# Experts of a mixture-of-experts stage: 28 pairs of token tiles with stationary weights, then 15 single tiles

## What is computed

```python
NUM_EXPERTS, TOP_K, HIDDEN, INTER = 8, 2, 256, 704
xf = layernorm(x).reshape(4096, HIDDEN)
top_w, sel = jax.lax.top_k(xf @ w_router.T, TOP_K)
top_w = jax.nn.softmax(top_w, axis=-1)
gates = zeros((4096, 8)).at[arange, sel].add(top_w)
for e in range(8):
    h = silu(xf @ w_gate[e]) * (xf @ w_up[e])
    out = out + gates[:, e:e + 1] * (h @ w_down[e])
x = x + out
```

## Time and profile before

| | |
|---|---|
| median of 3 runs | 1516.23 us |
| the profiled execution | 1514.07 us, span 1512.0 us |
| TensorE busy in the span | 1418.8 us (94%) |
| VectorE, ScalarE, GpSimd busy | 1119.2, 1002.8, 833.8 us |
| attention, scan and router | to 991 us |
| experts, first product to the end | 1003 to 1512 us |

### The profile page before, as it was taken

The page is one execution under the profiler, slowest core; times in us unless marked ns, Lnnn a source line. Parts: engine busy times, 40 slices in busy tenths (PEclk is TensorE's granted clock), DMA queues, the critical chain, the costliest instruction groups (busy, mean ns, idle before and its releaser), DMA issues.

```text
span 1512.0 us, 54304 instructions
## 1 busy us (share of the span) xinstructions
PE 1418.8 (94%) x15668; PEld 1285.3 (85%) x15669; DVE 1119.2 (74%) x3999; ACT 1002.8 (66%) x2482; POOL 833.8 (55%) x1401
## 2 busy tenths in 40 slices
PE   6969999999999999999999999559999999999997
PEld 5858888888888888888888888459999999999997
DVE  3647877877877877877877877558777777787775
ACT  4626777677777767767767766147767677677674
POOL 3514655655655665665665654236666656566554
PEclk9969999999999999999999999569999999999999
DMA  6202454454343343343343231425555555555554
GB/s 189 71 21 72 139 180 129 145 186 129 104 112 91 100 116 91 97 119 91 92 120 95 83 83 31 183 97 145 160 145 151 155 143 159 136 144 162 143 143 111
DMA packets 102009, 183.81 MB, mean 122 GB/s; under 512 B 19392, under 2 KB 61376, under 8 KB 101792
## 3 DMA queue, kind: packets, MB, share of 16 engines
q1 hardware_dynamic: 86272, 164.35, 35.8%
q0 software_dynamic: 15680, 18.76, 7.0%
HBM read 152.63 MB, written 31.13 MB: 122 GB/s over the span
## 4 chain that ended last, share of the span: by engine, by line
PE 70%; DVE 10%; issue 7%; DMA 2%; POOL 2%; ACT 1%; DVEq 1%; POOLq 0%; ACTq 0%; SPq 0%
PE k L412 12%; PE m L412 10%; PE y_p L1474 9%; PE up_p L1474 9%; PE gate_p L1474 8%; PE v_p L412 6%; PE sc L412 5%; PE v_p L476 4%; PE pt L476 3%; PE ht_p L1513 3%; DVE kT L873 2%; DMA par<-zbuf,gi 2%; PE m L497 2%; DVE z L1031 1%; PE z_p L1480 1%
## 5 line engine op out<-in xcount | busy, mean ns | idle before, releaser
L738 ACT ACTIVATE wd<-wd,nmx 128x257 f32<-128x257 f32 x512 | 256.3, 504 | 35.3 <-DVE nmx L884 30.6
L714 ACT ACTIVATE wd<-v_p 128x512 f32<-128x512 f32 x256 | 152.6, 596 | 180.8 <-PE k L412 146.3
L884 DVE CUSTOM_DVE_ANT_0 wd<-sc,wd 128x257 f32<-128x257 f32 x512 | 192.2, 423 | 74.2 <-PE sc L412 69.5
L1301 POOL TENSOR_TENSOR ctx_lo<-wd,ctx_hi 128x516 fp32r<-128x516 f32 x128 | 166.9, 1304 | 138.3 <-ACT ctx_hi L714 138.3
L1676 POOL DMA_INDIRECT out<-par,oi x71 | 113.6, 1599 | 144.8 <-ACT par L1582 140.0
L412 PE MATMUL k<-ctx_hi,wkh 128*128 128x256 f32 x512 | 159.0, 311 | 1.7 <-POOL ctx_lo L1301 1.4
L1553 ACT ACTIVATE uw_hi<-wu 128x1408 fp32r x71 | 98.4, 1385 | 83.7 <-PE up_p L1474 83.4
L1664 POOL COPY oi<-par 128x4 int32 x71 | 148.1, 2086 | 0.0
L1611 DVE TENSOR_TENSOR uw_lo<-wu,uw_hi 128x1408 fp32r<-128x1408 f32 x71 | 115.5, 1626 | 41.2 <-ACT uw_hi L1553 41.2
L412 PE MATMUL k<-ctx_lo,wkh 128*128 128x256 f32 x512 | 145.4, 284 | 0.0
L412 PE MATMUL k<-ctx_hi,wkl 128*128 128x256 f32 x512 | 144.7, 283 | 0.0
(11 more groups left out here) (200 smaller groups left out, 4719.2 us busy)
## 6 DMA issues: line engine op xcount, KB each, us to landing
dl<-d_low SPq DMA_DIRECT2D x71, 768.0 KB, 4.4
wd<-in_ctx SPq DMA_DIRECT2D x128, 258.0 KB, 2.8
wd<-in_mask SPq DMA_DIRECT2D x512, 32.1 KB, 1.8
wd<-in_wd SPq DMA_DIRECT2D x24, 256.0 KB, 3.0
d_high<-wd SPq DMA_DIRECT2D x24, 256.0 KB
d_low<-wd SPq DMA_DIRECT2D x24, 256.0 KB
wd<-d_high SPq DMA_DIRECT2D x8, 768.0 KB, 9.2
wg<-in_wg SPq DMA_DIRECT2D x8, 704.0 KB
```

Of the source, the lines that this page charges most:

```text
L714: return nc.scalar.activation(out, in_, ACT.Copy, **kw)
L738: nc.scalar.activation(pr[:, g, :], sm[:, g, :], ACT.Exp, bias=nmx[:, g:g + 1], scale=-1.0, accum_out=rsum[:, g:g + 1]).then_inc(exp_done, 1)
L884: V.tensor_tensor_reduce(sm[:, g, :], SC[g][:, 0:S], msk[:, b, :], -1.0, 3.0e38, ALU.add, ALU.min, nmx[:, g:g + 1]).then_inc(max_done, 1)
L1301: G.tensor_tensor(ctx_lo[:, b % 2], ctx[:, b], ctx_hi[:, b % 2].bitcast(F32), ALU.subtract).then_inc(lo_done, 1)
```

## The change

The 71 tiles become 28 pairs (NPAIR) of two tiles of one expert, and 15 single tiles (NSLOT) that are worked on as before. The planner finds for each expert how many pairs it has, takes the first 28, and lists what is left as single tiles: 25 VectorE steps, of which not all wait for the one in front, four small transposes and two copies.

For a pair, gate and up are computed with the weights stationary and the 256 rows of z streamed. The result is h already transposed, so h needs no transposes. It comes in six chunks: five of 128 channels with 12 matmuls of 256 columns for gate and up together in one PSUM bank, and a last one in which 64 gate and 64 up channels share one stationary operand (6 matmuls). There are three banks. For each chunk ScalarE takes silu (`silu2`), VectorE the product (`gate_up2`), ScalarE the high half of h (`high_h`), VectorE the low half (`low_h`). The weights of an expert are split once a pair, in parts: the first two chunks (`high_a`, `low_a`, 128x512 for gate and for up), chunks 2 to 4 (`high_b`, `low_b`, 128x768 each) and the short chunk (128x128 each), laid out with gate and up channels in turn. The down product runs as before for each half of a pair, 18 matmuls of 256 columns, in `down_pair`. The low half of w_down is loaded once a pair into one buffer (`load_pair`). Gathers and scatters stay at 128 rows, two a pair, with one copy of slot rows for both. y of a pair has one buffer for each half, and `take_y2` waits for the scatter of the pair before from that buffer, and for `oi` of its pair.

In the diff `body2` is written for TensorE, ScalarE and GpSimd; VectorE's has ScalarE's order with the low halves and products. Lines left out are the buffers, the split of the weights and changed names of semaphores.

```diff
...
-NSLOT = (TOK * TOPK + E * (P - 1)) // P
-assert NSLOT % 2 == 1
+NPAIR = (TOK * TOPK // P - E) // 2
+NSLOT = (TOK * TOPK + E * (P - 1)) // P - 2 * NPAIR
+NTILE = NPAIR + NSLOT
...
-        PLAN = 10
+        PLAN = 25
...
-            for k in range(2):
-                last = mm(M[0:1, (k + 1) * P:(k + 2) * P], tl[:, 3 + k:4 + k], ident)
+            for k in range(4):
+                last = mm(SC[0][0:1, k * P:(k + 1) * P], tl[:, 4 + k:5 + k], ident)
...
+                def step(ins, then=0):
                     k[0] += 1
                     ins.then_inc(plan, 1)
-                    if k[0] < PLAN:
-                        dve.wait_ge(plan, k[0])
+                    if then:
+                        dve.wait_ge(plan, then)
...
+                rows = SC[0][0:1, :].rearrange("p (k n) -> p k n", k=4)
+                V.tensor_copy(info[0:1, :, 0:NPAIR], rows[:, 0:2, 0:NPAIR]).then_inc(info_done, 1)
+                V.tensor_copy(info[0:1, :, NPAIR:NTILE], rows[:, 2:4, 0:NSLOT]).then_inc(info_done, 1)
...
+        def pairs(eng, body):
+            body(0, 0)
+            body(1, 1)
+            with eng.Fori(2, NPAIR - 2, 2) as p:
+                body(p, 0)
+                body(p + 1, 1)
+            body(NPAIR - 2, 0)
+            body(NPAIR - 1, 1)
...
+        def slot(s, k):
+            return 2 * s + k if k < 2 else k + 2
...
+            def turn_pair(p, s):
+                pe.wait_ge(zg_in[s], 32 * (turn(p, s) + 1))
+                at_least(pe, z_done, p)
+                for a in range(NH):
+                    for h in range(2):
+                        o = a * F2 + h * P
+                        last = nc.tensor.transpose(Z2[:, o:o + P], zg2[:, s, h, a * P:(a + 1) * P], ident)
+                last.then_inc(z_ready, 1)
...
+            def chunk(p, s, k):
+                if k == 0:
+                    pe.wait_ge(z_done, p + 1)
+                    pe.wait_ge(a_low, SPLIT_A * (p + 1))
+                if k == 2:
+                    pe.wait_ge(b_low, SPLIT_B * p + 2)
+                if k == FULL:
+                    pe.wait_ge(b_low, SPLIT_B * (p + 1))
+                at_least(pe, hf_done, FC * p + k - 2)
+                (zh, zl), (wh, wl) = zT2[s], w2
+                for side in range(1 if k == FULL else 2):
+                    o = 2 * k * P + side * P
+                    for c in range(NH):
+                        for j, (w, z) in enumerate(((wh, zh), (wh, zl), (wl, zh))):
+                            last = mm(G2[k % 3][:, side * F2:(side + 1) * F2], w[:, c, o:o + P], z[:, c, :],
+                                      c == 0 and j == 0, c == NH - 1 and j == 2)
+                last.then_inc(gu_ready, 1)
+            def down_pair(p, s):
+                e = nc.tensor.value_load(pair_expert(p), min_val=0, max_val=E - 1)
+                pe.wait_ge(h_low, FC * (p + 1))
+                pe.wait_ge(dl2_in, 16 * (p + 1))
+                for h in range(2):
+                    at_least(pe, yp_done, 2 * p + h - 1)
+                    for c in range(FC):
+                        r, at = rows_of(c), slot(s, c)
+                        hh, hl = (x[r, at, h * P:(h + 1) * P] for x in hT2)
+                        wh, wl = wd[r, bass.ds(e, 1), c, :].rearrange("p o n -> p (o n)"), dl2[r, c, :]
+                        for j, (a, b) in enumerate(((hh, wh), (hh, wl), (hl, wh))):
+                            last = mm(Y2[h], a, b, c == 0 and j == 0, c == FC - 1 and j == 2)
+                    last.then_inc(yp_ready, 1)
+            def body2(p, s):
+                chunk(p, s, 0)
+                chunk(p, s, 1)
+                if not (isinstance(p, int) and p == 0):
+                    down_pair(p - 1, 1 - s)
+                if final(p):
+                    turn_z(0, 0)
+                else:
+                    turn_pair(p + 1, 1 - s)
+                for k in range(2, FC):
+                    chunk(p, s, k)
...
+            turn_pair(0, 0)
             pe.wait_ge(wd_in, 16 * E)
+            pairs(pe, body2)
+            down_pair(NPAIR - 1, 1)
+            pe.wait_ge(info_done, 2)
...
+            def silu2(p, k):
+                r = rows_of(k)
+                act.wait_ge(gu_ready, FC * p + k + 1)
+                at_least(act, hf_done, FC * p + k)
+                nc.scalar.activation(sg2[r, :], G2[k % 3][r, 0:F2], ACT.Silu).then_inc(sg_done, 1)
+            def high_h(p, s, k):
+                r = rows_of(k)
+                act.wait_ge(hf_done, FC * p + k + 1)
+                if k < 2:
+                    if not (isinstance(p, int) and p < 2):
+                        act.wait_ge(yp_ready, 2 * p - 2)
+                else:
+                    at_least(act, yp_ready, 2 * p)
+                high(hT2[0][r, slot(s, k), :], hf[k % 2][r, :], h_high)
+            def take_y2(p, s, h):
+                act.wait_ge(yp_ready, 2 * p + h + 1)
+                act.wait_ge(oi_done, p + 1)
+                if not (isinstance(p, int) and p == 0):
+                    act.wait_ge(y_out, 16 * (2 * p + h - 1))
+                nc.scalar.activation(yb2[:, h, :], Y2[h], ACT.Copy, scale=oi[:, s, h, 2:3].bitcast(F32)
+                                     ).then_inc(yp_done, 1)
+            def body2(p, s):
+                begun = not (isinstance(p, int) and p == 0)
+                e = nc.scalar.value_load(pair_expert(p), min_val=0, max_val=E - 1)
+                if begun:
+                    silu2(p - 1, FULL)
+                    high_h(p - 1, 1 - s, FULL)
+                high_b(p, e, 0)
+                silu2(p, 0)
+                high_b(p, e, 1)
+                high_h(p, s, 0)
+                silu2(p, 1)
+                high_short(p, e)
+                high_h(p, s, 1)
+                if not final(p):
+                    high_a(p + 1)
+                if begun:
+                    take_y2(p - 1, 1 - s, 0)
+                    take_y2(p - 1, 1 - s, 1)
+                if final(p):
+                    take_z(0, 0)
+                else:
+                    high_z(p + 1, 1 - s)
+                for k in range(2, FULL):
+                    silu2(p, k)
+                    high_h(p, s, k)
...
+            high_a(0)
+            high_z(0, 0)
+            pairs(act, body2)
+            silu2(NPAIR - 1, FULL)
+            high_h(NPAIR - 1, 1, FULL)
+            act.wait_ge(info_done, 2)
             split_gate(0, 0)
...
+            def gate_up2(p, k):
+                r = rows_of(k)
+                dve.wait_ge(sg_done, FC * p + k + 1)
+                up_at = G2[k % 3][FL:P, 0:F2] if k == FULL else G2[k % 3][:, F2:2 * F2]
+                V.tensor_tensor(hf[k % 2][r, :], sg2[r, :], up_at, ALU.mult).then_inc(hf_done, 1)
+            def low_h(p, s, k):
+                r = rows_of(k)
+                dve.wait_ge(h_high, FC * p + k + 1)
+                low(hT2[1][r, slot(s, k), :], hf[k % 2][r, :], hT2[0][r, slot(s, k), :], h_low)
...
+            def pair_owners(dst, p, done):
+                col = G.value_load(info[0:1, 0, bass.ds(p, 1)], min_val=0, max_val=TCOL - 2)
+                G.tensor_copy(dst, tab[:, bass.ds(col, 2), :]).then_inc(done, 1)
+            def gather_pair(p, s):
+                if not (isinstance(p, int) and p < 2):
+                    pool.wait_ge(z_ready, p - 1)
+                pair_owners(gi[:, s], p, gi_done)
+                held(pool, (tab_in, 16), (gi_done, p + 1))
+                for h in range(2):
+                    G.indirect_dma_start(zg2[:, s, h, :], None, zbuf[:, :],
+                                         bass.IndirectOffsetOnAxis(gi[:, s, h, 0:1].bitcast(U32), 0)).then_inc(zg_in[s], 16)
+            def scatter_pair(p, s):
+                for h in range(2):
+                    held(pool, (tab_in, 16), (oi_done, p + 1), (yp_done, 2 * p + h + 1), (y_out, 16 * (2 * p + h)))
+                    G.indirect_dma_start(outd[:, :], bass.IndirectOffsetOnAxis(oi[:, s, h, 1:2].bitcast(U32), 0),
+                                         yb2[:, h, :], None, compute_op=ALU.add).then_inc(y_out, 16)
+            def body2(p, s):
+                if not (isinstance(p, int) and p >= NPAIR - 2):
+                    gather_pair(p + 2, s)
+                if isinstance(p, int) and p == NPAIR - 1:
+                    pool.wait_ge(info_done, 2)
+                    pool.wait_ge(z_ready, NPAIR - 1)
+                    gather(0, 0)
+                    gather(1, 1)
+                if not (isinstance(p, int) and p == 0):
+                    pair_owners(oi[:, 1 - s], p - 1, oi_done)
+                    scatter_pair(p - 1, 1 - s)
...
```

More of the change, by code:

```diff
@@ L1123, in plan_tiles @@
[L1123 to L1127, removed]
+                step(V.tensor_scalar(cnti[:, 0, :], M[:, 0:E], float(P - 1), None, ALU.add), 3)
@@ new lines, in plan_tiles @@
+                step(V.tensor_scalar(most[:, 1:E + 1], cum[:, 0, :], float(NPAIR), None, ALU.min))
+                step(V.tensor_scalar(past[:, 0, :], cum[:, 0, :], number, None, ALU.is_le), 10)
```

(58 more changed lines are left out.)

301 lines of the change are left out of this document (208 added, 93 removed).

## The result

The kernel after takes 1526.01 us (median of 6 runs, 1523.14 to 1528.99), the kernel before in the same comparison 1516.44 (6 runs): a ratio of 1.0069, 95% interval 1.0049 to 1.0088. It is slower by 0.7%, where 1487 was forecast, and it lies at the upper end of the stated range of 1474 to 1526. The profiled execution took 1528.4 us, with a span of 1526.6.

A forecast was written before the change was run, and what follows sets the result against it. TensorE was taken to bound the expert stage. 2.5 + 10.7 + 339.4 (27 pairs) + 0.4 + 4 + 13.3 + 98.0 (14 tiles) = 468.3 us against 497.4, -29.1, so 1487 us was predicted; range 1474 to 1526.

The forecast's parts named there:

- the sum: Expert stage, first expert product to last tile's h transposes: 497.4 us before, 468.3 after, a difference of -29.1.
- Gate and up, 102 matmuls at 0.119 and four transposes: TensorE's work for a pair, down included: 12.57 us, where two tiles took 13.74.
- The 6 products of the short chunk in down use 64 rows and are costed the same.: Down product of a pair: the 64-row matmuls were given the 256-column pitch of 0.119 us.
- the 32.8 us of gain: TensorE's saving over 28 pairs at 1.17 us each, from 12 transposes a pair that go.
- The chain of small steps: ScalarE and VectorE handing pieces back and forth: claimed to fit under TensorE's 12.57 us a pair, slack 0.3 to 0.6.
- The walk: Step-by-step timing of one ScalarE and VectorE round from silu of chunk 5 to the next, at 11.9 us.
- Rival B: The chain of small steps binds: rounds of 13.3 us, 28 x 0.7 = +20, 1507; range 1498 to 1512, chance 0.18.
- Occasional delays, 4 us: Occasional waits in the pairs, given 4 us (0 to 12), where the replaced tiles carried 7.1.
- GpSimd's queue, a round of 12.0: Scatters, gathers and copies from y to y: 10.9 to 13.3 us, taken as 12.0, below TensorE's 12.57.
- Start and first body: Before the pairs' steady part: first z +2.5 us, first body about 10.7 us, down of pair 0 waiting about 0.4.
- Seam, 13.3: From last pair to single tiles: gate 1 begins 12.6 us after the last chunk, 13.3 with slower clock; idle 2.5.

The follow-up runs named there:

- experiment 1: The kernel after, with the short chunk's h zero-padded so its down products use all 128 rows: 1507.86 us, ratio to before 0.995.
- experiment 7: The kernel after with full rows in down, gather of single tile 2 ahead of the last pair's scatters, silu 5 first, loop kept: 1485.42 us, ratio 0.9796.
- experiments 1 and 2: Against the kernel after: 1, full rows in the short chunk's down products, 1507.86 us; 2, 64-row matmuls spread, 12 switches a pair instead of 4, 1568.7 us.
- experiment 3: The kernel after with the 28 pair bodies written out on every compute engine instead of a loop: 1512.53 us, ratio to before 0.9971.
- experiment 5: The kernel after with the gather of single tile 2 issued ahead of the last pair's two scatters: 1523.13 us, ratio to before 1.0038.
- experiment 4: The kernel after with silu and product of chunk 5 ahead of chunk 4's high and low halves, loop kept: 1508.22 us, ratio to before 0.995.
- first kernel of experiment 6: The kernel after with full rows in down, gather of tile 2 moved ahead and no loop over pairs: 1488.39 us, ratio to before 0.982.

## Why the prediction was wrong

From the first chunk (1006.48) to the last tile's transposes (1515.1) the kernel after took 508.6 us, where the sum had 465.8 behind its start of 2.5. Of the miss of 42.8 us, 34.6 are the pairs with their delays, 1.9 the way across the seam to the second single tile's gate, 6.2 the single tiles behind it, 0.2 the first body. Step by step:

- **Gate and up, 102 matmuls at 0.119 and four transposes.** Right: 66 chunk matmuls took 7.91 us (0.120), and the best versions run at 12.59 and 12.60 against 12.57. With full rows and silu 5 early the kernel takes 1481.5 to 1485.4 us beside the forecast's 1487, so the sum fails by the terms below and not by this one.
- **"The 6 products of the short chunk in down use 64 rows and are costed the same."** The step that failed most. Their own time is the same, but the way in and out is not: 0.59 + 0.15 = 0.74 us a pair, 28 x 0.74 = 20.7 us. By itself it takes nearly two thirds of the 32.8 us of gain. The trace of before had no operand of 64 rows, so this was an unknown without a row; the text bounded the pitch of gate and up from both sides, and not this.
- **The chain of small steps, "slack of 0.3 to 0.6 us".** Wrong, and with the wrong critical member. The walk looked for the round's length, and that was never the limit: through the pairs ScalarE waited for VectorE's products 152 times, 0.5 us each. It put the low half of chunk 5 at 2.5 us after chunk 0 starts, needed at 2.85. Measured, silu 5 began 0.88 us after chunk 0 did, where the walk's 2.5 leave about 0.7, since it stood behind the high half of chunk 4, and that half took 0.42 us, not 0.38:

```profile
1214.83 0.42 ACT L1727 ACTIVATE room<-con 128x256 fp32r<-128x256 f32 x1 [0.49 <-DVE con L1909]
...
1215.52 0.38 ACT L1760 ACTIVATE con<-all_p 64x256 f32<-64x256 f32 x1 [0.27 <-issue]
...
1216.46 0.42 ACT L1727 ACTIVATE room<-con 64x256 fp32r<-64x256 f32 x1 [0.57 <-DVE con L1909]
...
1216.91 0.42 DVE L1880 TENSOR_TENSOR room<-con,room 64x256 fp32r<-64x256 f32 x1 [0.48 <-ACT room L1727]
...
1217.70 0.38 PE L1592 MATMUL all_p<-wd,room 128*128 x1 [0.18 <-issue]
```

  The low half ended at 1217.33, 2.69 us after chunk 0's start at 1214.64, and TensorE started 0.37 later, a handoff that the walk did not count. Down waited 0.18 and, started afresh, took 0.22 more than its 4.28 (4.50 in experiment 1, while 102 matmuls in a stream take 12.15, 36 of them 4.29): 0.40 us a pair, 27 x 0.40 = 10.8. The row for the high half was the earlier trace rows's 256-wide one, whose source was PSUM; h's comes from SBUF, and the 400 ns of the Trainium skill's table (VectorE: DVE Perf Modes, "The TRN2 errata"), which the text had set aside, was the nearer figure to the measured 418.
- **The loop's turn.** Not in the sum at all. VectorE's register loads, branch and the instructions on both sides of it stood in that chain for 1.1 us (from 1229.1 to 1230.2 in the chain shown first); 0.56 us of it reached the path, 12 times, 6.7 us. Rival B had the place right (down waiting for low halves), and its 0.7 us a pair stands beside a measured 0.40 + 0.28 = 0.68. That is luck in the size: B's 0.7 was for a round made longer by slower handoffs between ScalarE and VectorE, with ScalarE never idle, and neither was seen. What was seen is one late half and the loop's turn, and they came beside the switches.
- **Occasional delays, 4 us.** Did not come; behind the first pair TensorE waited for no pair's gather.
- **GpSimd's queue, a round of 12.0.** In the kernel after it isn't reached: bodies of 14.02 hide it, and GpSimd stood waiting for y 92.6 us. The direction was right, the size 0.6 to 0.8 short: 12.62 and 12.83 in turn once TensorE needs only 12.59 (experiment 7).
- **Start and first body.** 10.9 us for the forecast's 10.7; down of pair 0 waited 1.0, not 0.4. The first product came 3.5 us later than before (1006.48 against 1003.0), where the sum had 2.5. What of this is the planning's 15 more steps can't be told: the first transposes began at 1003.9, and in the profiles of the kernels here, which share all that stands in front of them, between 1001.1 and 1005.1.
- **Seam, 13.3.** 15.2 to the second single tile's gate. The idle was 2.56 us (forecast 2.5), and the clock fell behind it, which cost 1.55 us in the first half of down alone; the text had put half of 1.4 on it. Behind it came the gather of tile 2, queued behind two scatters: the text named that order for the pairs and not at the seam, where it cost 5.6 us of idle.

All terms together: 20.0 (switches, 27 pairs) + 10.8 + 6.7 = 37.5, less the 4 us of delays that did not come, plus 0.6 at down 0, is 34.1 of the 34.6.

Left open: what TensorE does during the 0.34 to 0.37 us after VectorE's low half is done inside the loop. Unlooped and at the seam it is 0.13, so it goes with the loop, but no run separated wait, branch and value load. Open too is what decides whether the clock falls at the seam.

## What to carry to other kernels

An operand shape that the trace has never shown gets its own bound, and not only for its duration but for the switch into and out of it: pad a short stationary operand to the rows of its neighbours if TensorE sets the pace. When work is cut in small pieces that pass between engines, compute for each consumer when its last piece is ready, with the order on each queue as written, and put that order right (here one silu moved ahead was worth 18 us of 1526, and 7 where rows and loop had been mended already) before trusting a slack of a few tenths. A loop's turn on an engine inside such a chain is a term of the sum.

## What the runs showed of the hardware

- Between stationary operands of 128 and of 64 rows TensorE loses 0.197 us at each change (experiments 1 and 2); each load by itself takes 0.19 us.
- A loop turn on VectorE with its register loads takes about 1.1 us (1229.1 to 1230.2 in the first chain); the two longest pieces, on the line that loads the expert's number, take 0.31 and 0.19 us.
- VectorE to TensorE: 0.34 to 0.37 us from end to start inside the loop, 0.13 outside (experiment 3 and the seam).
- At the same place, in front of the last pair's down product, the granted clock fell behind an idle of 2.56 us in two kernels (experiment 5) and behind 2.12 us in the kernel of experiment 4, and stayed at 1.00 behind 2.56 us in the first kernel of experiment 6 and behind 2.12 us in that of experiment 7, whose 48 matmuls took 6.46:

```profile
1364.33 6.46 PE all_p L1592 x48
```

- An operation on 256 columns takes ScalarE 0.42 us from SBUF (418 ns, the high half of h) and 0.38 from PSUM (376 ns, silu).
